# Adjacency layers on one core: rounds of 4, 6, 8, 8 and 14 row tiles, two narrow column blocks first, row sums of x in the head

## What is computed

```
u = par_u[0] * par_u[1] * (diag_u[:, None] * ego_u @ W_u) + ego_u      # rows 0..2047
i = par_i[0] * par_i[1] * (diag_i[:, None] * ego_i @ W_i) + ego_i      # rows 2048..5119
e = concatenate([u, i])
h = adj @ (adj.T @ e)
out = (h - mu) * rsqrt(var + LN_EPS) * ln_gamma + ln_beta + res
x = _layernorm(x + out)
x = _layernorm(x + message layers(x, adj))      # two pruning layers
```

## Time and profile before

| | us |
|---|---|
| median of three runs | 415.06 |
| lowest, highest | 414.40, 415.21 |
| profiled execution, its own time | 414.27 |
| its span in the trace | 412.5 |

### The profile page before, as it was taken

One profiled execution on the slowest core, in us unless ns is written; L12 is line 12 of the kernel. 1 busy time (PEld: TensorE's weight loads), 2 busy tenths in 40 slices (PEclk: granted clock), 3 DMA queues, 4 the chain that ended last, 5 costly groups with the idle time before them and its releaser, 6 DMA issues.

```text
span 412.5 us, 13885 instructions
## 1 busy us (share of the span) xinstructions
PE 383.8 (93%) x6018; PEld 223.2 (54%) x6018; DVE 324.7 (79%) x404; ACT 266.6 (65%) x497; POOL 68.6 (17%) x122
## 2 busy tenths in 40 slices
PE   8987999999999999999999999999999999999940
PEld 7543555565464455546445554644555464668740
DVE  3699769799695979769786966988696697694783
ACT  3696938799888488578848857884785688100220
POOL 2001100303003000300200030011003001169663
PEclk9999999999999999999999999999999999999995
DMA  8999999954992998399389929957992995400002
GB/s 293 386 387 381 386 386 387 382 217 144 388 386 109 322 387 314 114 388 385 138 289 379 354 83 373 387 184 260 385 370 55 392 386 202 130 4 3 29 27 82
DMA packets 56706, 109.87 MB, mean 266 GB/s; under 512 B 3776, under 2 KB 3904, under 8 KB 56640
## 3 DMA queue, kind: packets, MB, share of 16 engines
q1 hardware_dynamic: 56352, 108.84, 72.6%
q10 hardware_dynamic: 288, 0.09, 0.1%
HBM read 107.60 MB, written 1.31 MB: 264 GB/s over the span
## 4 chain that ended last, share of the span: by engine, by line
PE 51%; DMA 23%; SPq 18%; DVE 2%; issue 2%; POOL 1%; ACT 0%; DVEq 0%; ACTq 0%
PE pair L1382 39%; DMA pooled<-in_adj 22%; SPq L977 17%; PE pair L1363 10%; PE pair L1395 2%; DMA pooled<-in_x 2%; POOL pooled L1052 1%; DVE pooled L1204 1%; SPq L968 1%; DVE pooled L1182 1%; SPq L963 1%; POOL pooled L1047 0%; DVE pooled L1272 0%; DVE pooled L1264 0%; DVE pooled L1293 0%
## 5 line engine op out<-in xcount | busy, mean ns | idle before, releaser
L1086 ACT ACTIVATE scratch<-pooled 128x1024 bf16<-128x1024 f32 x200 | 210.5, 1053 | 63.8 <-DMA pooled<-in_adj 61.9
L1182 DVE STREAM_TRANSPOSE pooled<-pooled 128x1024 f32<-128x1024 f32 x200 | 228.8, 1208 | 11.3 <-ACT scratch L1086 8.9
L1363 PE MATMUL pair<-pooled,rows_in 128*64 128x256 f32 x1600 | 186.0, 383 | 10.7 <-DMA pooled<-in_adj 10.3
L1382 PE MATMUL pair<-pooled,col_sum 32*64 32x320 f32 (+3 forms) x4224 | 177.4, 485 | 0.9 <-DVE pooled L1204 0.5
L1363 PEld LDWEIGHTS pair<-pooled,rows_in 128*64 128x64 f32 x1600 | 109.6, 137 | 88.4 <-DMA pooled<-in_adj 31.1
L1382 PEld LDWEIGHTS pair<-pooled,col_sum 32*64 32x64 f32 x4224 | 94.0, 132 | 78.7 <-issue 57.0
L1204 DVE TENSOR_TENSOR pooled<-pooled,pair 128x320 f32<-128x320 f32 (+3 forms) x120 | 58.1, 545 | 44.6 <-PE pair L1382 44.6
L1022 POOL COPY col_sum<-col_half 32x256 f32<-32x256 f32 x80 | 31.6, 394 | 317.6 <-DVE col_half L1191 314.6
L1095 ACT COPY col_sum<-col_half 32x256 f32<-32x256 f32 x80 | 32.2, 403 | 11.1 <-DVE col_half L1191 10.3
L1086 ACT ACTIVATION_READ_ACCUMULATOR scratch<-pooled 128x1 f32 x200 | 37.4, 187 | 0.0
L1113 ACT ACTIVATE pooled<-pair 128x512 f32<-128x512 f32 x5 | 3.0, 598 | 39.3 <-PE pair L1395 39.3
(11 more groups left out here) (47 smaller groups left out, 62.2 us busy)
## 6 DMA issues: line engine op xcount, KB each, us to landing
pooled<-in_adj SPq DMA_DIRECT2D x200, 512.0 KB, 10.1
pooled<-in_x SPq DMA_DIRECT2D x5, 256.0 KB, 3.7
out<-pooled SPq DMA_DIRECT2D x5, 256.0 KB, 2.0
pooled<-in_x SPq DMA_DIRECT2D x1, 768.0 KB, 6.9
pooled<-in_x SPq DMA_DIRECT2D x1, 512.0 KB, 3.7
pooled<-in_w_ui ACTq DMA_DIRECT2D x1, 64.0 KB, 2.9
beta_sb<-in_beta SPq DMA_DIRECT2D x1, 32.0 KB, 9.0
pooled<-in_scales ACTq DMA_DIRECT2D x1, 22.0 KB, 3.2
```

Source lines behind the costliest of these rows:

```text
L1086: nc.scalar.activation(scratch[v % 2][:, :], slots[slot_of(v)], ACT.Square, accum_out=square_sum[:, v:v + 1]).then_inc(unit_scanned, 1)
L1182: nc.vector.transpose(tiles, tiles).then_inc(unit_turned, 1)
L1363: mm = pe.matmul(block_bank[c % 2][half(h), 0:w // 2], rows_in[:, t, :], slots[slot_of(v)][:, at:at + w // 2], start=(t == 0), stop=(t == ...
L1382: mm = pe.matmul(round_banks(g)[a][half(b % 2), 0:w].rearrange("p (t r) -> p t r", r=32), col_sum[c % 2][quadrant(a), b, :], to[quadrant(a ...
```

## The change

- Two blocks of 256 columns come first, then nine of 512. A unit of a narrow block holds four row tiles of 256 columns, so it is 512 KB as before, in rows of 1 KB instead of 2 KB. The two narrow blocks have 10 units each, in slots 20 to 29 and 30 to 39, and rounds of 8, 16 and 16 row tiles, all in banks 0 to 3. Their rounds are put among the units that come in.
- The blocks of 512 columns have rounds of 4, 6, 8, 8 and 14 row tiles, the last but one 6, 10, 10 and 14; the last has 5 x 8 as before.
- The row sums of x are made in the head from the first copy of x (five reductions `sum_x` between the steps of `make_e`) and kept in a tile of their own. The reduction over x in the tail is gone, and GpSimd makes all five `center_x` before the first `root_c`.

```diff
-    WIDTHS = (512,) * 10
+    WIDTHS = (256, 256) + (512,) * 9
-    SLOT_FIRST = [20 if c % 2 == 0 else 0 for c in range(NB)]
+    SLOT_FIRST = [20, 30] + [0 if c % 2 == 0 else 20 for c in range(2, NB)]
-    PARTS = [((0, 10), (10, 14), (24, 16))] * (NB - 2)
-    PARTS += [tuple((t, 10) for t in range(0, T, 10)), tuple((t, 8) for t in range(0, T, 8))]
+    PARTS = [((0, 8), (8, 16), (24, 16))] * 2
+    PARTS += [((0, 4), (4, 6), (10, 8), (18, 8), (26, 14))] * (NB - 4)
+    PARTS += [((0, 6), (6, 10), (16, 10), (26, 14)), tuple((t, 8) for t in range(0, T, 8))]
...
-            return c > 0 and (g - ROUNDS_AT[c]) % 2 == 1
+            return c > 1 and (g - ROUNDS_AT[c]) % 2 == 1
...
                     sp.wait_ge(e_made, LGROUPS)
+                    sp.wait_ge(x_summed, LGROUPS)
...
-            for k in range(LGROUPS - 1):
+            for k in range(LGROUPS):
                 center_x(k)
+            pool.wait_ge(x_steps, 1 + 3 * LGROUPS)
             root_c(0)
-            pool.wait_ge(rstd_made, 1)
-            center_x(LGROUPS - 1)
-            pool.wait_ge(x_steps, 1 + 3 * LGROUPS)
...
+            def sum_x(k):
+                dve.wait_ge(x_loaded[k], 16)
+                nc.vector.tensor_reduce(x_sum[:, group_tiles(k)], x_first[:, group_tiles(k), :], X,
+                                        ALU.add).then_inc(x_summed, 1)
+            sum_x(0)
...
-                    dve.wait_ge(x_again, 16 * 2)
-                    nc.vector.tensor_reduce(x_sum[:, :], x_all[:, :, :], X, ALU.add).then_inc(x_summed, 1)
```

More of the change, by code:

```diff
@@ L113, in adjacency_layers_kernel @@
         x_all = pooled[:, x_at:x_at + T * D].rearrange("p (t d) -> p t d", d=D)
-        x_sum, c_sum, var, rstd, y_sum, y_var, y_eps, x1_rstd, scale = (
-            pooled[:, x_at + T * D + T * i:x_at + T * D + T * i + T] for i in range(9))
-        ln_at = x_at + T * D + 9 * T
+        c_sum, var, rstd, y_sum, y_var, y_eps, x1_rstd, scale = (
+            pooled[:, x_at + T * D + T * i:x_at + T * D + T * i + T] for i in range(8))
+        ln_at = x_at + T * D + 8 * T
         def ln_buffer(i):
@@ L137, in adjacency_layers_kernel @@
         beta_sb = sb("beta_sb", [P, D])
+        x_sum = sb("x_sum", [P, T])
         beta_sum = sb("beta_sum", [P, 1])
@@ L1106, in _ @@
                     keep_cols(c)
-                if c == 1 and i == UPB[c] // 2:
+                if c == 2 and i == UPB[c] // 2:
                     act.wait_ge(gamma_turned, 1)
@@ L1205, in add_round @@
                 added.then_inc(round_added, 1)
+            sum_x(1)
             make_e(0)
             make_e(1)
+            sum_x(2)
             make_e(2)
-            for v in range(3):
-                turn_unit(v)
+            turn_unit(0)
+            sum_x(3)
             make_e(3)
-            for v in range(3, 7):
-                turn_unit(v)
+            turn_unit(1)
+            sum_x(4)
             make_e(4)
-            for v in range(7, UPB[0] - 2):
+            for v in range(2, 6):
                 turn_unit(v)
             turn_half(0)
-            for v in range(UPB[0] - 2, UPB[0]):
+            for v in range(6, 9):
                 turn_unit(v)
-            for g in rounds_of(0):
-                for v in units_of(1, *place_of_round(g)[1:]):
+            add_round(0)
+            for v in range(9, 12):
+                turn_unit(v)
+            add_round(1)
+            for v in range(12, 14):
+                turn_unit(v)
+            add_round(2)
+            for v in range(14, 16):
+                turn_unit(v)
+            turn_half(1)
+            for v in range(16, 20):
+                turn_unit(v)
+            for g in rounds_of(1):
+                for v in units_of(2, *place_of_round(g)[1:]):
                     turn_unit(v)
-                if g == ROUNDS_AT[1] - 1:
-                    turn_half(1)
+                if g == ROUNDS_AT[2] - 1:
+                    turn_half(2)
                 add_round(g)
-                if g == 0:
+                if g == ROUNDS_AT[1]:
                     make_gamma_and_beta()
-            for c in range(1, NB - 1):
+            for c in range(2, NB - 1):
                 first = UNIT_FIRST[c + 1]
@@ L1418, in _ @@
                     multiply_unit(v)
-            for g in rounds_of(0):
-                for v in units_of(1, *place_of_round(g)[1:]):
+            for v in range(10, 12):
+                multiply_unit(v)
+            multiply_round(0)
+            multiply_unit(12)
+            multiply_round(1)
+            for v in range(13, 15):
+                multiply_unit(v)
+            multiply_round(2)
+            for v in range(15, 20):
+                multiply_unit(v)
+            for g in rounds_of(1):
+                for v in units_of(2, *place_of_round(g)[1:]):
                     multiply_unit(v)
                 multiply_round(g)
-                if g == 1:
+                if g == ROUNDS_AT[1] + 1:
                     pe.wait_ge(gamma_made, 1)
```

35 lines of the change are left out of this document (22 added, 13 removed).

## The result

| | before | after |
|---|---|---|
| median of four runs, us | 414.73 | 453.39 |
| lowest, highest | 412.41, 415.21 | 450.34, 458.21 |
| profiled execution, its own time | 414.27 | 455.03 |
| its span | 412.5 | 452.9 |

The ratio is 1.092, 95% interval 1.0831 to 1.1009; the run of 458.21 us had a lower granted clock (0.934, the others 0.972 to 0.980) and is not in it. The prediction was 404.4 us with a range up to 412: wrong in sign and far outside the range.

The account below looks back on a forecast made before the run. Late-starting adj loads, waiting for slots that the rounds release, were taken as the bound. Terms -11.6 + 0.2 + 1.5 - 0.8 = -10.7 us gave 403.6 profiled, 404.4 us median; range 401.5 to 412.

Parts of the forecast that it names:

- The period, -11.6 us: Blocks of rounds and units: an earlier first release cuts seven periods from 256.5 to 244.9 us, 34.9 each.
- The two added rounds of a block thus cost 0.1 us: Step of the period term: five rounds cost little more than three, as rounds in one go have a small fixed part.
- The line for short rounds: Rounds of 4 and 6 tiles: 0.427 us per tile plus a fixed part; 1.75 us for 4, about 2.6 for 6.
- The earlier release: Wide blocks: slots first released at T+1.75 after the rounds' start T, first unit at T+6.0, twentieth at T+32.8.
- a stop per block: Rival, chance 0.16: TensorE stops for instruction fetches in each block, 7 x 0.7 us, giving 409.3 us.
- 27 ns a matmul: Rival, chance 0.10: least time per matmul makes rounds of 4 and 6 cost 2.55 us more a block; 423.1 us.
- Weight loads: Rival, chance 0.06: weight loads bound the short rounds, 1.4 us a block, giving back 10.2; 414.6 us.
- The head, +0.2: Before the third block's rounds: 1 KB packets cost 1.0 us, offset by slack between 91.5 and 92.34.
- the late turn, +1.5: Behind the head: VectorE turns the sum late, delaying the second round once by 1.5 us, from 0 to 3.
- the 0.8 us of slack: Head: time to be won between the sixtieth unit multiplied at 91.5 and the third block's rounds at 92.34.
- The tail, -0.8: Tail: without the reduction over x, TensorE's 0.52 us stop at 370.20 and its restart go, saving 0.8 us.

Follow-up runs that it names:

- the small loads: The kernel after, but from the fifth block on a unit's load brings 64 KB instead of 512 KB, leaving out most of adj; one run, 417.88 us.
- The kernel with the old rounds: The kernel after, with rounds of 10, 14 and 16 tiles back in its wide blocks; median 415.44 us, ratio 1.0012 to the kernel before.

## Why the prediction was wrong

**The period, -11.6 us.** The step that failed is "The two added rounds of a block thus cost 0.1 us". It priced a round by its columns and a fixed part, and not by its 256 instructions. The starts of the rounds, 95.55 to 390.45 in the timeline, make seven periods of 42.13 us instead of 34.9: 7.2 us a block that the sum didn't have, 50.6 in all. By the waits and windows of the seven blocks of rounds, 32.2 of them are stops for instructions (4.6 a block) and 0.9 the wait for VectorE. The other 17.5 are longer busy time: 1.7 a block at full clock (1.3 with the small loads, with hardly a stop), where the sum had 0.1, and nearly 6 in all by the lower clock.

The line for short rounds holds with its fixed part: 2.01 us for 4 tiles, where 4 x 0.427 + 0.22 is 1.93; the 1.75 of the sum took the smaller fixed part of rounds in one go. The earlier release worked at first: with T = 178.59 the first unit is scanned at 185.09, T+6.5, where the forecast was T+6.0. The twentieth is scanned only at 218.79, T+40.2 instead of T+32.8, since the stops hold back the later releases: the last comes at T+27.2, and 27.2 + 4.2 + 6 x 1.41 is 39.9. The DMA of `adj` left the chain all the same, because the period had grown to 42.1. So this kernel does not show that the release at T+1.75 alone would have freed the rounds.

**The rival "a stop per block"** had the right mechanism, from the right rows: 49 fetches, 246 instructions each, and the stop at 391.28. Its size was wrong: 0.7 us a block, where stops took 4.6 and the whole loss was 7.2. It took the length of a stop from the tail, where no load of `adj` runs, and counted one or two in a block. There are two to four in each (24 with the tail's, up to 3.4 us), and loads of `adj` run beside them. The numbers for it stood in the earlier trace rows: while loads ran, the kernel before used 256 instructions in 4.49 us at the fastest, and never that fast for more than one piece. A rate twice as high was outside everything seen beside loads, and the rival had no price for that.

**The rival "27 ns a matmul"** falls: 128 matmuls in 2.01 us are 16 ns each. The Trainium skill (TensorE: Matmul & The Clock Gate, "Wait — 56ns, not 53.3ns?") says that start to start never drops below about 25 ns; with these 32 x 64 tiles in four quadrants the trace does not agree. **Weight loads** as a bound fall with the same number.

**The head, +0.2, and the late turn, +1.5.** The third block's rounds began at 95.55 instead of the 92.5 expected, 3.2 us after the start of before. The timeline of TensorE, after:

```profile
94.54 1.08 PE L1392 MATMUL pair<-pooled,rows_in 128*64 128x256 f32 x8 [1.20 <-DMA pooled<-in_adj]
95.55 2.10 PE L1411 MATMUL pair<-pooled,col_sum 32*64 32x128 f32 x128
98.54 1.72 PE L1411 MATMUL pair<-pooled,col_sum 32*64 32x192 f32 x72 [0.89 <-DVE pooled L1191]
```

The sixtieth unit came late, and the 1 KB packets account for most of it. In the slices of the page above DMA moved 349 and 349 GB/s in the second and third, while narrow units came, and 387 where rows are of 2 KB. The twenty narrow units are 10.5 MB; at 349 instead of 387 they take 2.9 us longer (30.0 for 27.1), where the term had 1 us. With the 0.8 us of slack that it counted on, and that wasn't won, that is 2.7 of the 3 (an estimate from these slices). The Trainium skill (DMA: Bandwidth & Descriptors, Specifications) sets the least transfer at line rate at 512 bytes. By these rates the trace does not agree for rows of 1 KB. The late turn was there: the second round waited 0.89 us for VectorE. The term was 1.5.

**The tail, -0.8.** From the ninth block's rounds to the end it is 62.5 us (452.9 - 390.45) after 63.7 (412.5 - 348.82), so -1.2, with one stop of 0.96 in it.

The parts add up: 3.2 for the start of the third block, 294.9 - 256.5 = 38.4 for seven periods, -1.2 for the tail: 40.4, the span's difference. The kernel with the old rounds bears out that the rest of the change is worth nothing: 2.4 more in its head (94.72 against 92.34), 1.0 more in its seven periods, and a tail 1.5 shorter.

## What to carry to other kernels

Cutting the same work into more instructions has a price beyond their fixed cost: where a stretch uses TensorE's instructions faster than they come in, it stops. Here, beside the loads of `adj`, 640 matmul records in 17.5 us of work stopped in every block, 512 in some, and 384 in none. Count the instructions of a stretch beside its columns, and compare the rate with the fastest that the kernel already bears. To release buffers earlier and more evenly, mix the two kinds of work before making either smaller, and follow the order to its last block, where the gain of the steady part can be lost once.

## What the runs showed of the hardware

- TensorE's instructions come in pieces of 16 KB, 245 to 249 instructions by the counts of four kernels (49, 64, 74 and 48 fetches), and stops fall 127 or 128 matmul records apart. The Trainium skill (Runtime: NRT & Kernel Launch, "Instruction fetch mechanics") has the 16 KiB blocks of 256 instructions, and the trace agrees. It also calls the cost of crossing one "mostly hidden" and gives TensorE room for 2048 instructions. The first holds for the kernel before (one stop of 0.41 us) and not for the kernel after (33.3 us).
- The traces do not agree with the room for 2048. They have the start of each fetch on queue 8. In all thirteen kernels fetch n, counted from 0, begins when TensorE has started 256n + 155 to 256n + 449 of the matmuls, weight loads and semaphore instructions that the trace has (the last one or two fetches aside), and 449 is the highest value in each of the five kernels that stop most. That fits two pieces in store, 512 instructions of which the trace lacks some, with the next piece fetched when one is used up. However long the units leave, 17.4 us for 320 instructions, the store ahead of a block of rounds is no larger: the first stop behind 178.59 comes after 154 matmuls, some 308 instructions.
- Pieces follow each other 3.5 to 4.1 us apart with DMA almost idle (share 0.18), and 4.4 to 7.4 us apart while `adj` is loaded (share near 0.8), where TensorE stops for each. The fetch itself takes 1.0 us on average beside the loads and 1.1 us with the small ones.
- A limit on the loads in flight recovers 1.7 of 7.7 us a block. Why the next fetch comes so late beside other traffic, and whether another placing of the loads would spare it, was not tried.
